# A graph network's kernel: VectorE's long operations tied to the beginning of scatters, and new cells ranked within their scatter pass

## What is computed

```python
h = max(layernorm(x), 0); x = x + L0(h)   # Gaussian mixture: sum over edges of (h @ g)[src] * gauss(attr), mean at dst
h = max(layernorm(x), 0); x = x + L1(h)   # two mean aggregations with dense layers (SAGE)
h = max(layernorm(x), 0); x = x + L2(h)   # spline convolution, below
h = max(layernorm(x), 0); x = x + L3(h)   # two sum aggregations with dense layers (SAGE)

# in L2, after a small network gave every node an offset t of three numbers:
new = clip(attr + t[col] - t[row], 0, 1)
i0, frac = floor and rest of new * 4           # the cell of an edge: one of 64
z = sum over 8 corners of basis(frac) * h[col] @ W[cell corner]
out = segment_sum(z, row) / degree + bias
```

## Time and profile before

| | us |
|---|---|
| median of 3 runs (lowest, highest) | 10463.64 (10461.68, 10470.80) |
| the profiled execution | 10493.68 |
| its span | 10491.6 |

### The profile page before, as it was taken

How to read it: one execution, slowest core, us unless ns; L and a number is a source line. 1 busy time by engine, 2 the same in 40 slices (tenths; PEclk the granted TensorE clock), 3 DMA queues, 4 the chain that set the end, 5 groups by cost and what they waited for, 6 DMA issues and landing times. The chain is left out here.

```text
span 10491.6 us, 187901 instructions
## 1 busy us (share of the span) xinstructions
PE 6169.3 (59%) x48488; PEld 5174.2 (49%) x48489; DVE 6368.4 (61%) x19749; ACT 2334.7 (22%) x6546; POOL 6325.7 (60%) x6534
## 2 busy tenths in 40 slices
PE   5444056665777766666456576655554555546575
PEld 5443045554777754444445555334444444445454
DVE  8996086664666659999547665731111544458565
ACT  0000034443333322222104040011111222204040
POOL 3777637776777767777434146257776777724151
PEclk9999988887555558888567575655555555557575
DMA  6990012222433322222395566680000111136565
GB/s 210 302 201 7 26 44 86 85 85 76 115 104 106 104 71 62 65 66 66 65 231 209 125 224 158 134 100 17 14 14 11 35 34 34 34 74 239 111 224 113
DMA packets 1315188, 1070.73 MB, mean 102 GB/s; under 512 B 894004, under 2 KB 1157417, under 8 KB 1306047
## 3 DMA queue, kind: packets, MB, share of 16 engines
q1 hardware_dynamic: 954526, 693.52, 25.9%
q0 software_dynamic: 225216, 300.54, 8.7%
q10 hardware_dynamic: 135264, 74.60, 3.1%
HBM read 518.16 MB, written 591.91 MB: 106 GB/s over the span
## 5 line engine op out<-in xcount | busy, mean ns | idle before, releaser
L2822 POOL DMA_INDIRECT msg<-row,idx x1792 | 1758.1, 981 | 608.5 <-issue 524.8
L1179 POOL DMA_INDIRECT run_rows<-rec,idx x544 | 632.1, 1162 | 1320.2 <-ACT rec L1157 1174.3
L2581 POOL DMA_INDIRECT cell<-rec,idx x944 | 919.9, 974 | 504.6 <-issue 284.3
L2392 POOL DMA_INDIRECT cell<-rec,idx x944 | 966.8, 1024 | 334.0 <-issue 286.8
L2047 POOL DMA_INDIRECT rec_d<-rec,idx x880 | 872.5, 991 | 454.0 <-issue 267.0
L516 POOL DMA_INDIRECT rec_r<-sc_rec,sc_idx x832 | 830.1, 998 | 431.0 <-issue 283.5
L2803 PE MATMUL ps<-w_stn,hft 128*128 x1792 | 609.6, 500 | 365.2 <-ACT hft L2731 341.5
L837 DVE TENSOR_TENSOR oh<-iota_f,rd 128x128 f32<-128x128 f32 x948 | 217.8, 289 | 951.4 <-PE ps L2503 950.6
L1137 PE MATMUL ps<-planes,hot 128*128 x8704 | 568.0, 224 | 334.4 <-DVE hot L1119 172.0
L2518 PE MATMUL ps<-h_rows,oht 128*128 x1888 | 450.9, 403 | 525.2 <-ACT oht L2525 524.9
L1119 DVE TENSOR_SCALAR hot<-loc,lane_c 128x512 bf16<-128x512 bf16 x2176 | 662.7, 382 | 123.9 <-PE ps L1137 66.1
(11 more groups left out here) (448 smaller groups left out, 15754.3 us busy)
## 6 DMA issues: line engine op xcount, KB each, us to landing
loc<-loc_s SPq DMA_DIRECT2D x68, 2048.0 KB
got<-run_rows SPq DMA_DIRECT2D x472, 224.0 KB
got<-rec_d SPq DMA_DIRECT2D x236, 416.0 KB
rec_d<-padd SPq DMA_DIRECT2D x4, 12480.0 KB
rec_d<-padd SPq DMA_DIRECT2D x4, 12064.0 KB
msg<-zpad SPq DMA_DIRECT2D x8, 5390.0 KB
got<-msg SPq DMA_DIRECT2D x220, 196.0 KB
cin<-cell SPq DMA_DIRECT2D x224, 136.0 KB, 2.2
```

The lines of the kernel that those rows point to most:

```text
L1179: nc.gpsimd.indirect_dma_start(out=out, out_offset=bass.IndirectOffsetOnAxis(ap=idx[:, u, m % HU:m % HU + 1], axis=0), in_=rec[:, m, :], i ...
L2392: nc.gpsimd.indirect_dma_start(out=cells, out_offset=bass.IndirectOffsetOnAxis(ap=idx[:, n, g:g + 1], axis=0), in_=rec[:, n, g, :], in_off ...
L2581: nc.gpsimd.indirect_dma_start(out=cells, out_offset=bass.IndirectOffsetOnAxis(ap=idx[:, n, g:g + 1], axis=0), in_=rec[:, n, g, :], in_off ...
L2822: nc.gpsimd.indirect_dma_start(out=msgs, out_offset=bass.IndirectOffsetOnAxis(ap=idx[:, m, g:g + 1], axis=0), in_=row[:, m, g, :], in_offs ...
```

## The change

Five scattering passes get a semaphore `begun`. POOL first adds a credit to it (24 in the first stage, G * LAG or the like in the others: 32, 28, 16; in send_runs 5) and then 1 behind every scatter's issue. VectorE waits on it before its long operations, for a count that grows with the batch k, and these operations come in one piece. In `rank_position` the multiplication stands before the "upto" addition. Ranking of new cells moves into `to_cells` with J = 1 (14 matmuls a batch), and what remains of `place_cells` is a count, with the normalisation's operations between the marks. Blanking of cell2 moves behind that of run_rows, beside `sum_messages(msg1)`. Shown are the added and removed lines that matter, with their common indentation taken off.

```diff
@@ tally_marks @@
-for b in range(bins):
+for b in bins:
...
@@ rank_hot, rank_position @@
-def rank_hot(v, s, key, k, m):
-    shape = [P, s["J"], G // len(s["parts"]), CELLS]
+def rank_hot(v, s, key, k, m, begun, count):
+    shape = [P, s["J"], G, CELLS]
-    for B in s["parts"]:
-        made = nc.vector.tensor_tensor(s["hot"][:, m, :, B, :], bcast(iota_f[:, 0:CELLS].unsqueeze(1).unsqueeze(1), shape),
-                                       bcast(key[:, :, B].unsqueeze(3), shape), ALU.is_equal)
-    made.then_inc(s["s_hot"], 1)
-def rank_position(v, s, to, k, m):
+    v.wait_ge(begun, count)
+    nc.vector.tensor_tensor(s["hot"][:, m, :, :, :], bcast(iota_f[:, 0:CELLS].unsqueeze(1).unsqueeze(1), shape),
+                            bcast(key.unsqueeze(3), shape), ALU.is_equal).then_inc(s["s_hot"], 1)
+def rank_position(v, s, to, k, m, begun, count):
+    v.wait_ge(begun, count)
+    nc.vector.tensor_tensor(sel, sel, s["hot"][:, m, :, :, :], ALU.mult).then_inc(s["s_sel"], 1)
-    for B in s["parts"]:
-        taken = nc.vector.tensor_tensor(sel[:, :, B, :], sel[:, :, B, :], s["hot"][:, m, :, B, :], ALU.mult)
-    taken.then_inc(s["s_sel"], 1)
...
@@ first ranking stage: scatter_pool and its rings @@
+AHEAD_OF_SCATTERS = 3 * 2 * GN // G
-                fed=sem_in(c, "fed"), sent=[sem_in(c, f"sent{n}") for n in range(2)])
+                fed=sem_in(c, "fed"), begun=sem_in(c, "begun"), sent=[sem_in(c, f"sent{n}") for n in range(2)])
...
+nc.gpsimd.sem_inc(s["begun"], AHEAD_OF_SCATTERS)
...
+nc.gpsimd.sem_inc(s["begun"], 1)
...
@@ first stage: LATE @@
-NG, LATE = EJ // STEP, 18
+NG, LATE = EJ // STEP, 21
...
@@ first stage: the calls @@
-rank_hot(v, ranks, keys[:, :, ds(j, G)], k, m)
+rank_hot(v, ranks, keys[:, :, ds(j, G)], k, m, rings["begun"], 3 * k + 1)
...
-rank_position(v, ranks, raw[:, :, n * G:(n + 1) * G], i * R + n, n)
+rank_position(v, ranks, raw[:, :, n * G:(n + 1) * G], i * R + n, n, rings["begun"], 3 * (i * R + n) + 5)
...
@@ send_runs (LAG = 5) @@
+v.wait_ge(s_begun, k + 1)
-    for e in (slice(0, HR * P), slice(HR * P, RUN * P)):
-        made = nc.vector.tensor_scalar(hot[:, m % RING, w, e], loc[:, u, m % HU, e], lane_c[:, w:w + 1], None,
-                                       ALU.is_equal)
+    made = nc.vector.tensor_scalar(hot[:, m % RING, w, :], loc[:, u, m % HU, :], lane_c[:, w:w + 1], None,
+                                   ALU.is_equal)
...
@@ source pass (LAG = 5 + AHEAD = 8, credited G * LAG) @@
+nc.gpsimd.sem_inc(s_begun, 1)
...
@@ source pass: spread and weigh @@
-quarters = [slice(q * UB, (q + 1) * UB) for q in range(G)]
-    for T in quarters:
-        made = nc.vector.tensor_tensor(diff[:, T, :, :], bcast(rrt[:, u, T, RATT:RATT + KD].unsqueeze(2), [P, UB, KG, KD]),
-                                       bcast(mu_b[:, :].rearrange("p (k d) -> p k d", d=KD).unsqueeze(1), [P, UB, KG, KD]),
-                                       ALU.subtract)
-    made.then_inc(s_diff, 1)
+    nc.vector.tensor_tensor(diff[:, :, :, :], bcast(rrt[:, u, :, RATT:RATT + KD].unsqueeze(2), [P, TURN, KG, KD]),
+                            bcast(mu_b[:, :].rearrange("p (k d) -> p k d", d=KD).unsqueeze(1), [P, TURN, KG, KD]),
+                            ALU.subtract).then_inc(s_diff, 1)
-    for T in quarters:
-        made = nc.vector.tensor_tensor(diff[:, T, :, :], diff[:, T, :, :],
-                                       bcast(inv[:, :].rearrange("p (k d) -> p k d", d=KD).unsqueeze(1), [P, UB, KG, KD]),
-                                       ALU.mult)
-    made.then_inc(s_scaled, 1)
+    nc.vector.tensor_tensor(diff[:, :, :, :], diff[:, :, :, :],
+                            bcast(inv[:, :].rearrange("p (k d) -> p k d", d=KD).unsqueeze(1), [P, TURN, KG, KD]),
+                            ALU.mult).then_inc(s_scaled, 1)
...
@@ source pass: hot and basis @@
-hots_by_tile(oh[:, m % RING, :, :], rrt[:, u, T, RLOC]).then_inc(s_hot, 1)
+v.wait_ge(s_begun, G * k + 1)
+hot_of(oh[:, m % RING, :, :], rrt[:, u, T, RLOC]).then_inc(s_hot, 1)
-for g in range(G):
-    made = nc.vector.tensor_tensor(basis[:, m % RING, g, 0:KW].rearrange("p (a b) -> p a b", b=KS),
-                                   bcast(pair[:, m % 2, g, :].unsqueeze(2), [P, KS * KS, KS]),
-                                   bcast(h[:, g, 2, :].unsqueeze(1), [P, KS * KS, KS]), ALU.mult)
-made.then_inc(s_basis, 1)
+v.wait_ge(s_begun, G * k + 2)
+nc.vector.tensor_tensor(basis[:, m % RING, :, 0:KW].rearrange("p g (a b) -> p g a b", b=KS),
+                        bcast(pair[:, m % 2, :, :].unsqueeze(3), [P, G, KS * KS, KS]),
+                        bcast(h[:, :, 2, :].unsqueeze(2), [P, G, KS * KS, KS]), ALU.mult).then_inc(s_basis, 1)
...
@@ destination pass (LAG = 4, AHEAD = 3, credited G * (LAG + AHEAD)) @@
-hots_by_tile(oh[:, n % RING, :, :], got[:, n, :, XW + MLOC]).then_inc(s_hot, 1)
+v.wait_ge(s_begun, G * k + 1)
+hot_of(oh[:, n % RING, :, :], got[:, n, :, XW + MLOC]).then_inc(s_hot, 1)
-for g in range(G):
-    made = nc.vector.tensor_tensor(prod[:, n % 2, g, :].rearrange("p (k o) -> p k o", k=KG), picked[:, g, :, :],
-                                   bcast(by[:, g, :].unsqueeze(2), [P, KG, C]), ALU.mult)
-made.then_inc(s_prod, 1)
+v.wait_ge(s_begun, G * (k + AHEAD) + 2)
+nc.vector.tensor_tensor(prod[:, n % 2, :, :].rearrange("p g (k o) -> p g k o", k=KG), picked,
+                        bcast(by.unsqueeze(3), [P, G, KG, C]), ALU.mult).then_inc(s_prod, 1)
...
@@ pick_pe, before the picks @@
+rank_batch(pe, ranks, k, n)
...
@@ pick_hot (LAG = 3) @@
-def pick_hot(v, s, k, t, n):
+def pick_hot(v, s, k, t, n, begun, count):
-    hots_by_tile(s["oh"][:, n, :, :], rd[:, ds(t, G), LOC]).then_inc(s["hot"], 1)
-def to_cells(nodes, pitch, F, cells, load_weights, blank):
+    v.wait_ge(begun, count)
+    one_hot(s["oh"][:, n, :, :], rd, t, LOC).then_inc(s["hot"], 1)
+def to_cells(nodes, pitch, F, cells, load_weights, blank, base):
+    LAG = 3
+        ranks = rank_rings(c, 4, base)
+        pos, pos_i, lane, tile = (sb_in(c, n, [P, G], dt) for n, dt in (("pos", F32), ("pos_i", I32), ("lane", I32), ("tile", I32)))
+        s_row, s_idx, s_begun = (sem_in(c, n) for n in ("row", "indexed", "begun"))
...
@@ to_cells, VectorE and TensorE @@
-pick_hot(v, s, 0, 0, 0)
-with v.Fori(0, NID) as i:
+def index(i, k, t, n, first):
+    rank_position(v, ranks, pos[:, :].unsqueeze(1), k, n, s_begun, G * k + G + 3)
+    v.wait_ge(ranks["s_pos"], k + 1)
+    nc.vector.tensor_tensor(pos_i[:, :], pos[:, :], rd[:, ds(t, G), ATT], ALU.add).then_inc(s_row, 1)
+    v.wait_ge(s_row, 3 * k + 1)
+    nc.vector.tensor_scalar(lane[:, :], pos_i[:, :], P - 1, None, ALU.bitwise_and).then_inc(s_row, 1)
+    nc.vector.tensor_scalar(tile[:, :], pos_i[:, :], 7, None, ALU.arith_shift_right).then_inc(s_row, 1)
+    v.wait_ge(s_row, 3 * k + 3)
+    if not first:
+        v.wait_ge(sent[n], 16 * G * i)
+    nc.vector.scalar_tensor_tensor(out=idx[:, n, :], in0=lane[:, :], scalar=float(TC), in1=tile[:, :],
+                                   op0=ALU.mult, op1=ALU.add).then_inc(s_idx, 1)
+def turn(i, first):
-        pick_hot(v, s, i * R + n + 1, i * STEP + (n + 1) * G, (n + 1) % R)
+        k, t = i * R + n, i * STEP + n * G
+        pick_hot(v, s, k + 1, t + G, (n + 1) % R, s_begun, G * (k + 1) + 1)
+        rank_hot(v, ranks, rd[:, ds(t + G, G), ROWC].unsqueeze(1), k + 1, (n + 1) % R, s_begun, G * (k + 1) + 2)
+        index(i, k, t, n, first)
+pick_hot(v, s, 0, 0, 0, s_begun, 1)
+rank_hot(v, ranks, rd[:, 0:G, ROWC].unsqueeze(1), 0, 0, s_begun, 2)
+turns(v, NID, turn)
-pick_pe(pe, s, nodes, F, pitch, filled)
+rank_start_pe(pe, ranks)
+pick_pe(pe, s, nodes, F, pitch, filled, ranks)
...
@@ to_cells, ScalarE @@
-nc.scalar.copy(idx[:, n, :], rd[:, ds(t, G), ROWC])
...
@@ to_cells, POOL @@
+nc.gpsimd.sem_inc(s_begun, G * (LAG + 1))
+        pool.wait_ge(s_idx, i * R + n + 1)
+            nc.gpsimd.sem_inc(s_begun, 1)
...
@@ count_cells in place of place_cells @@
-blank_tables(act, s_blank, blank)
+act.wait_ge(s_var, 1)
+nc.scalar.activation(std[:, :], var[:, :], ACT.Sqrt).then_inc(s_std, 1)
-sort_pe(pe, w, CELLS)
+tally_pe(pe, w, CELLS)
-sort_consts(then, w)
+def marks(b0, b1):
+    tally_marks(v, w, key_b[:, :], range(b0, b1))
-sort_dve(v, then, w, key_b[:, :], CELLS, CELLS, TC, rd[:, T, ROWC], "c2")
+marks(0, 8)
+then(nc.vector.memset(h_nm[:, :, C:C + 1], 1.0))
+then(nc.vector.tensor_reduce(m[:, :], x_nm[:, :, :], AX.X, ALU.add))
+marks(8, 14)
+then(nc.vector.tensor_scalar(m[:, :], m[:, :], 1.0 / C, None, ALU.mult))
+then(nc.vector.tensor_tensor(d[:, :, :], x_nm[:, :, :], bcast(m[:, :].unsqueeze(2), [P, NB, C]), ALU.subtract))
+marks(14, 20)
+then(nc.vector.tensor_tensor(sq[:, :, :], d[:, :, :], d[:, :, :], ALU.mult))
+marks(20, 26)
+then(nc.vector.tensor_reduce(var[:, :], sq[:, :, :], AX.X, ALU.add))
+nc.vector.tensor_scalar(var[:, :], var[:, :], 1.0 / C, 1e-5, ALU.mult, ALU.add).then_inc(s_var, 1)
+marks(26, 32)
+v.wait_ge(s_std, 1)
+then(nc.vector.reciprocal(r[:, :], std[:, :]))
+marks(32, 38)
```

(12 more changed lines are left out.)

45 lines of the change are left out of this document (25 added, 20 removed).

## The result

The changed kernel takes 10573.95 us (median of 4 runs, 10572.40 to 10580.49) against 10462.66 us before (median with a fourth run beside the three of the table above): the ratio is 1.0107 with a 95% interval of 1.0089 to 1.0124, so it is slower, by 111 us. The direction is the forecast's, the size a third of it (+355). It is nearest to rival B's 10539, but by accident: B's mechanism, waits that align and a cell pass bound by its ring, isn't what happened here.

A forecast was written before the change was run, and what follows sets the result against it. POOL's scatters, 1.277 us each, bound the passes, and waited whole operations would lengthen them. 149 + 157 − 5 + 0 − 107 + 66 + 95 = +355 on 10463.64 gives 10819 us, own range 10650 to 10950, 8 in 10: 10340 to 10930.

The forecast's parts named there:

- rival B: Waits align, but the cell pass is bound by its ring at half clock: +75 us, 10539 us; chance 0.17.
- ring: Cell pass: one-hot, transposes, rank matmuls, VectorE's part in turn; 5.9 us a batch at half clock, 4.5 at full, POOL 5.11.
- The step of the increment: POOL signals in the gap between scatters; a waiting operation starts 0.15 us before the next and lengthens it by 0.41 us.
- the sum (+157): Source pass: waited one-hot 0.41 and basis 0.38 us over 220 batches, 174 us less the 17 of excess there.
- First ranking: 208 batches, waited mult 0.41 and one-hot 0.37 us, every one exposed: 162 less 13 us of excess, +149.
- Cell pass: Whole one-hot holds a scatter by 0.40 us in each of 236 batches: +95; ring alone 0 to +186.
- Sending runs: 4 × 136 scatters beside one-piece tensor_scalar on bf16 with one SBUF input: wait and pieces about 0, bounds -10 and +20.
- Destination pass: Phases set by the landings as now; one whole prod may hold one scatter longer or miss it: -5, bounds -49 and +47.
- Placing: Place cells: copy_predicated, separate normalisation and work around the loop go, marks and normalisation are added: net -107, bounds -120 and -90.
- blanking: Blanking of cell2 moves behind run_rows' parts and is exposed in the sum_messages stage: +66, bounds +30 and +85.
- Rival A: Waits align and operations start just after the scatter: -111 us, 10353; chance 0.28, and 0.12 for a milder form (10420).
- C: Waits don't bind or phases drift; a whole operation costs 0.10 us: +15, no change; chance 0.06.

The follow-up runs named there:

- micro: Separate kernel without the graph, short phases of scatters beside VectorE operations: a scatter takes 1.37 us beside a waited whole one-hot, 0.97 undisturbed.
- rank_first: Changed kernel with TensorE counting batch k before turning batch k + 1's one-hot in the cell pass: 12427.98 us, 0.9831 of the kernel before.
- src_free: Changed kernel with a credit of 900 in the source pass, so its waits on begun never bind, operations whole: 0.9870 of the kernel before.

## Why the prediction was right in sign and wrong in size

The step of the increment was right: it is signalled in the gap, the waiting operation starts 0.16 (micro) to 0.24 us (source pass) before the scatter and lengthens it by 0.32 to 0.40 us, as L816 and L831 had done by chance. For the source pass the sum (+157) was 33 us too high, by the start alone: working it with 0.24 in place of 0.15 gives 0.32 + 0.31 a batch, 139 us, less the 17: 122, against +124.

What failed first is one assumption, made for two stages: that every waiting operation is exposed to a scatter's start because of its wait.

- First ranking, +149 against +28. The step was "hot and mult each wait, ... and every waiting operation is exposed". The wait on POOL ended VectorE's idle time 21 times, TensorE's count 139 times. Of 204 recorded multiplications 103 crossed a start, and their scatters were lengthened by 34 us in all (the term was 85); the one-hots cost 13 (the term was 77). A wait that is already met when VectorE comes to it sets no phase; only one multiplication was released by it, so the phase of the others came from the operations before them. That the one-hot with its computed address starts nearer the scatter was right: of the 21 that the wait released, 11 began 0.042 to 0.044 us before a scatter and cost nothing, 5 began 0.045 to 0.055 before and cost 0.51 to 0.52.
- Cell pass, +95 against +12. The +95 were the whole one-hot held to a start in each of 236 batches. No wait on begun bound, and 1 of 235 recorded one-hots crossed a start; most began 0.8 to 1.2 us before the next one. The multiplication and the one-hot of 256 elements, which the ranking brought in, cost 10 and 3 us. The ring was not the limit either, so my 5.9 us for it were too long: between two scatters there were the usual 0.305 us, in the whole pass 1 us more, and 944 × (0.986 + 0.305) = 1219 is the pass. The ring took at most these 5.16 us a batch. The clock was 0.50 as assumed,

```profile
6990.00:8208.00 1218.00, 838.87 (x6110) 792.92 (x6110) 684.40 (x2350) 208.30 (x704) 929.18 (x943) 0.50 0.21 32
```

  (the cell pass in the changed kernel; columns as in the earlier trace rows), and TensorE's busy time grew from 662 to 839 us, 0.75 us a batch, where I had 1.7 for the 14 matmuls: they overlap more than the busy time of one at full clock, doubled, says. Where TensorE's instructions came late, the pass grew by 240 us and rank_first took 133 of them away. Rival B named the place and the mechanism, and had its price for the wrong condition.
- Sending runs, 0 against -45. Two steps failed: that the 90 us of excess in the four passes are "all that a better placing of VectorE's work can win", and that one SBUF input makes these operations harmless. The row of L1179, at a mean of 1162 ns, holds 544 × 0.190 = 103 us more. They sit in two scatters of each call: 11 to 20 us at its start and 4 to 15 in its middle. After the change the excess is 69 us (mean 1099), which gives 34 of the 45; idle time between the scatters gives the other 11. One view in order of time would have shown the chain of 96.
- Destination pass, -5 against +19. prod in one piece did what was hoped (its crossings cost 9 us instead of 40), but the whole one-hot ran across a start in 214 of its 231 records and cost 59 us instead of 9. It is the same size as in the source pass, and I had no term for it: "the phases are set by the landings as now" left out that a longer operation at a start costs more. POOL released it 57 times, the landing of `got` 104 times and TensorE 66 times, and nearly all of each kind crossed. Why the last two kinds also come before a start is open.
- Placing -107 (-114) and blanking +66 (+62) came out nearly by their own working. The 64 marks took 36 us instead of 45, and the eight new parts of the blanking were issued 11 us apart, from 5623.5 to 5700.8, behind the last message loads.

Rival A fell with the rows of the source pass; C is what src_free shows, 0.10 us for each whole operation at a drifting phase. The Trainium skill's sentence (SBUF — State Buffer, "Who interferes with whom") that tensor_tensor does not hold up descriptor generation is not borne out: 1.37 against 0.97 us in micro. The same section's rule that copies, casts and tensor_scalar operations in two-port modes can contend with GpSimd was the one to weigh for the sending runs; the scatters of 19.76 and 14.34 us beside tensor_scalar on bf16 agree with it. I had left it out.
